# A gated cross-attention and quantised feed-forward block on one core: the variance and the joined statistics placed ahead of the last maximum, the roots kept in two buffers, the split alternated with longer operations, and the context halves turned at other places

## What is computed

```python
# attention: the mask and the shapes leave one key per query, so softmax is 1
x = x + tanh(g_xattn) * ((context @ Wv) @ Wout + bout)
# feed-forward, per token
h = layernorm(layernorm(x), ln1_g, ln1_b)
h = act_quant(h) @ weight_quant(w1).T + b1        # 256 -> 1024
h = gelu(h)
h = layernorm(h, ln2_g, ln2_b)
h = act_quant(h) @ weight_quant(w2).T + b2        # 1024 -> 256
x = x + tanh(g_ffn) * h
```

## Time and profile before

| what | value |
|---|---|
| median of 3 runs | 412.6 us (412.28 to 414.04) |
| the profiled execution | 411.33 us, span 409.5 us |
| busy: DVE, PE, ACT, POOL | 327.3 (80%), 309.5 (76%), 277.6 (68%), 221.4 (54%) us of the span |
| mean granted TensorE clock | 0.946 of full speed |

### The profile page before, as it was taken

The page is one execution under the profiler, slowest core; times in us unless marked ns, Lnnn a source line. Parts: engine busy times, 40 slices in busy tenths (PEclk is TensorE's granted clock), DMA queues, the critical chain, the costliest instruction groups (busy, mean ns, idle before and its releaser), DMA issues.

```text
span 409.5 us, 5758 instructions
## 1 busy us (share of the span) xinstructions
PE 309.5 (76%) x1658; PEld 186.5 (46%) x1658; DVE 327.3 (80%) x794; ACT 277.6 (68%) x446; POOL 221.4 (54%) x117
## 2 busy tenths in 40 slices
PE   2846777687969697979797969797979684938365
PEld 2744643343636363636363636363636341515043
DVE  0345461998999999999999999999999996968681
ACT  1202237598887878787888888787878776969421
POOL 4000416577566666666666666666666666664600
PEclk9988889998999999999999999999999996969688
DMA  7941223316365555556555555555552526353625
GB/s 225 378 149 47 81 91 108 89 51 115 117 116 169 113 170 112 171 104 182 108 175 107 178 105 179 103 179 104 128 101 81 101 79 88 93 96 86 153 53 154
DMA packets 98557, 51.59 MB, mean 126 GB/s; under 512 B 87407, under 2 KB 89640, under 8 KB 98526
## 3 DMA queue, kind: packets, MB, share of 16 engines
q1 hardware_dynamic: 96608, 51.00, 49.1%
q10 hardware_dynamic: 1918, 0.23, 0.4%
HBM read 21.78 MB, written 8.46 MB: 74 GB/s over the span
## 4 chain that ended last, share of the span: by engine, by line
DVE 41%; PE 30%; issue 12%; POOL 7%; DMA 5%; ACT 3%; DVEq 0%; POOLq 0%; ACTq 0%
DVE y L657 10%; PE bank_f L904 8%; POOL rstd L295 6%; PE slot_c L864 5%; DVE h L616 5%; DVE amax L624 5%; DVE res L707 5%; PE slot_a L890 4%; DVE amax L661 3%; DMA split_vectors<-vec_parts 3%; PE slot_b L890 3%; DVE x L573 2%; DVE parts L559 2%; PE slot_a L887 2%; PE bank_q L794 2%
## 5 line engine op out<-in xcount | busy, mean ns | idle before, releaser
L311 POOL TENSOR_TENSOR y<-u,g_bc 128x1024 f32<-128x1024 f32 x64 | 150.2, 2369 | 28.7 <-DVE parts L559 25.4
L295 POOL TENSOR_TENSOR rstd<-var,half_neg 128x8 f32<-128x8 f32 x18 | 30.3, 1683 | 129.5 <-DVE var L698 86.1
L657 DVE TENSOR_TENSOR y<-y,slot_c 128x1024 f32<-128x1024 f32 x64 | 77.6, 1212 | 5.0 <-PE slot_c L864 5.0
L661 DVE TENSOR_REDUCE amax<-y 128x1 f32<-128x1024 f32 x64 | 78.1, 1220 | 2.2
L441 ACT ACTIVATE junk<-u,usum 128x1024 bf16<-128x1024 f32 x64 | 73.7, 1151 | 1.2
L414 ACT ACTIVATE q<-y,s 128x1024 f16<-128x1024 f32 x64 | 69.8, 1139 | 5.2 <-DVE s L688 5.0
L843 PE MATMUL bank_q<-wvo,ctxT 128*128 128x256 f32 x256 | 69.1, 402 | 0.0
L904 PE MATMUL bank_f<-w2T,q2T 128*128 128x256 f16 x512 | 64.1, 281 | 0.0
L904 PEld LDWEIGHTS bank_f<-w2T,q2T 128*128 128x128 f16 x512 | 51.5, 101 | 14.3 <-issue 0.8
L405 ACT ACTIVATE q<-h,s 128x256 f16<-128x256 f32 x64 | 27.3, 496 | 41.2 <-DVE s L648 41.1
L864 PE MATMUL slot_c<-ln_rows,rows 128*128 128x512 bf16 x128 | 40.9, 402 | 16.9 <-DVE y L657 8.5
(11 more groups left out here) (104 smaller groups left out, 393.1 us busy)
## 6 DMA issues: line engine op xcount, KB each, us to landing
c_in<-in_ctx SPq DMA_DIRECT2D x16, 512.0 KB, 3.3
x_in<-in_x SPq DMA_DIRECT2D x16, 512.0 KB, 4.6
out<-res SPq DMA_DIRECT2D x32, 256.0 KB, 2.4
y<-in_L_ffn_w SPq DMA_DIRECT2D x2, 1024.0 KB, 12.1
u<-in_L_xattn_Wkv SPq DMA_DIRECT2D x1, 1024.0 KB, 7.0
u<-in_L_xattn_Wout SPq DMA_DIRECT2D x1, 1024.0 KB, 10.6
q2T<-q SPq DMA_TRANSPOSE x64, 3.3
g_bc<-in_L_ffn_ln_g SPq DMA_DIRECT2D x1, 512.0 KB, 12.4
```

The costliest lines, as they stand in the source:

```text
L295: nc.gpsimd.tensor_tensor(rstd[:, :, :], var[:, :, :], half_neg[:, :, :], ALU.pow) \
L311: nc.gpsimd.tensor_tensor(y[:, k % 2, t, :], u[:, t, :], g2_bc[:, :], ALU.mult).then_inc(gain2_done, 1)
L657: nc.vector.tensor_tensor(line, line, slot_c[:, :], ALU.add).then_inc(y_done, 1)
L661: nc.vector.tensor_reduce(amax2[:, t:t + 1], y[:, k % 2, t, :], AX.X, ALU.max, apply_absolute_value=True).then_inc(amax2_done, 1)
```

## The change

On DVE, `variance` works on block i at the end of body i, in place of block i-1 at the start of the next one. It and all of `join(i+2)` stand ahead of the maximum `first(i+1, 0)`, and the joins no longer lie among the steps of `first` and `second`. `rstd` has two buffers, `root(i+1)` is issued at the end of POOL's body i, and `deviations` is the first thing in a DVE body. The five splits alternate with residual, statistics and final operations. `final` is cut into single tiles, and those of block i-2 come after the fourth `row_max` in place of ahead of the fourth `row`. On PE the context half 0 is turned ahead of `hidden(0)`, half 1 after `shift_first`; `correction(3)` stands ahead of `second_product(i-2, 0)`. ACT copies half 0 ahead of `gelu(1)` and half 1 after `square(3)`.

```diff
-        rstd = sb("rstd", [P, 2, T])
+        rstd = sb("rstd", [P, 2, 2, T])
...
-                def root():
-
-                    wait(pool, var1_done, min(i + 2, S))
-                    wait(pool, var2_done, i)
-                    wait(pool, first_ready, min(i + 1, S))
-                    wait(pool, second_ready, i - 1)
+                def root(j):
+
+                    wait(pool, var1_done, min(j + 2, S))
+                    wait(pool, var2_done, j)
+                    wait(pool, first_ready, min(j, S))
+                    wait(pool, second_ready, j - 2)
...
                 if -1 <= i <= S:
-                    root()
                     wait(pool, split_steps, split_count(i))
...
+                if -1 <= i + 1 <= S:
+                    root(i + 1)
...
                 if live(i):
                     gelu(0)
                     square(0)
-                    gelu(1)
                 if live(i + 3) and i > -3:
                     take_context(i + 3, 0)
                 if live(i):
+                    gelu(1)
                     square(1)
                     gelu(2)
-                if live(i + 3) and i > -3:
-                    take_context(i + 3, 1)
-                if live(i):
                     square(2)
                     gelu(3)
                     square(3)
+                if live(i + 3) and i > -3:
+                    take_context(i + 3, 1)
...
                 def variance(k):
 
                     wait(dve, square_done, T * k + T)
-                    wait(dve, split_steps, split_count(k))
+                    wait(dve, std_done, i + 2)
+                    wait(dve, split_steps, split_count(i))
...
-                def final(k, pair):
-
-                    wait(dve, ffn_done, T * k + 2 * pair + 2)
-                    if pair == 0:
+                def final(k, t):
+
+                    if t % 2 == 0:
+                        wait(dve, ffn_done, T * k + t + 2)
+                    if t == 0:
                         wait(dve, stored[k % 2], 32 * (k // 2))
...
-                if live(i - 1):
-                    variance(i - 1)
+                splitting = -1 <= i <= S + 1
+                if -1 <= i <= S:
+                    deviations()
+                if splitting:
+                    split(0)
                 if live(i + 2):
                     residual(i + 2, 0)
+                if splitting:
+                    split(1)
+                if live(i + 2):
                     statistics(i + 2, 0)
...
-                if -1 <= i <= S:
-                    deviations()
-                if -1 <= i <= S + 1:
-                    for n in range(5):
-                        split(n)
+                if splitting:
+                    split(2)
+                if live(i + 2):
+                    statistics(i + 2, 1)
+                if splitting:
+                    split(3)
                 if live(i - 3):
-                    final(i - 3, 1)
+                    final(i - 3, 2)
+                if splitting:
+                    split(4)
+                if live(i - 3):
+                    final(i - 3, 3)
                 if live(i + 2):
                     residual(i + 2, 1)
-                    statistics(i + 2, 1)
+                    statistics(i + 2, 2)
+                    statistics(i + 2, 3)
...
-                if live(i - 2):
-                    final(i - 2, 0)
                 if live(i - 1):
                     row(i - 1, 3)
                     row_max(i - 1, 3)
+                if live(i - 2):
+                    final(i - 2, 0)
+                    final(i - 2, 1)
                 if live(i + 1):
                     shift_first(i + 1)
+                for n in range(4):
+                    if live(i + 2):
+                        join(i + 2, n)
+                if live(i):
+                    variance(i)
+                if live(i + 1):
                     first(i + 1, 0)
                 for n in range(4):
...
                     if live(i + 1):
                         first(i + 1, n + 1)
-                    if live(i + 2):
-                        join(i + 2, n)
...
+                if live(i + 3) and i > -3:
+                    turn_context(i + 3, 0)
                 if live(i):
                     hidden(0)
...
-                if live(i + 3) and i > -3:
-                    turn_context(i + 3, 0)
...
                 if live(i):
                     hidden(2)
+                if live(i - 1):
+                    correction(i - 1, 3)
                 if live(i - 2):
                     second_product(i - 2, 0)
-                if live(i + 3) and i > -3:
-                    turn_context(i + 3, 1)
-                if live(i - 1):
-                    correction(i - 1, 3)
                 if live(i):
                     hidden(3)
                 if live(i + 1):
                     shift_first(i + 1)
+                if live(i + 3) and i > -3:
+                    turn_context(i + 3, 1)
                 if live(i - 2):
                     second_product(i - 2, 1)
```

More of the change, by code:

```diff
@@ L288, in body @@
             def body(i):
-                def root():
-                    wait(pool, var1_done, min(i + 2, S))
-                    wait(pool, var2_done, i)
-                    wait(pool, first_ready, min(i + 1, S))
-                    wait(pool, second_ready, i - 1)
-                    nc.gpsimd.tensor_tensor(rstd[:, :, :], var[:, :, :], half_neg[:, :, :], ALU.pow) \
+                def root(j):
[3 more added lines that the diff above has]
+                    wait(pool, second_ready, j - 2)
+                    nc.gpsimd.tensor_tensor(rstd[:, j % 2, :, :], var[:, :, :], half_neg[:, :, :],
+                                            ALU.pow) \
                         .then_inc(rstd_done, 1)
@@ L541, in deviations @@
                     wait(dve, split_steps, split_count(i - 1))
-                    nc.vector.tensor_tensor(stat[:, 1:4:2, :], var[:, :, :], rstd[:, :, :], ALU.mult) \
+                    nc.vector.tensor_tensor(stat[:, 1:4:2, :], var[:, :, :], rstd[:, i % 2, :, :],
+                                            ALU.mult) \
                         .then_inc(std_done, 1)
@@ L577, in residual, with statistics @@
                         .then_inc(x1_done, 1)
[L579 to L585, removed]
+                def statistics(k, t):
+                    if t % 2 == 0:
+                        wait(dve, x1_done, 2 * k + t // 2 + 1)
+                        wait(dve, join_steps, 3 * k)
+                    op = nc.vector.bn_stats(bn[:, t, :], x1[:, k % SETS, t, :])
+                    if t == T - 1:
+                        op.then_inc(bn_done, 1)
                 def join(k, n):
                     if n == 0:
-                        wait(dve, bn_done, 2 * k + 2)
-                        wait(dve, split_steps, split_count(k - 2))
+                        wait(dve, bn_done, k + 1)
+                        wait(dve, std_done, i + 2)
+                        wait(dve, split_steps, split_count(i))
                         nc.vector.tensor_tensor(mean1[:, :], bn[:, :, 1], bn[:, :, 4], ALU.add)
@@ L627, in first @@
                         wait(dve, first_steps, 4 * k + 1)
-                        nc.vector.tensor_tensor(amax1_g[:, :], amax1[:, :], rstd[:, 0, :], ALU.mult) \
-                            .then_inc(first_steps, 1)
+                        nc.vector.tensor_tensor(amax1_g[:, :], amax1[:, :], rstd[:, i % 2, 0, :],
+                                                ALU.mult).then_inc(first_steps, 1)
                     elif n == 2:
@@ L648, in first @@
                         nc.vector.scalar_tensor_tensor(
-                            out=s1[:, :], in0=amax1_inv[:, :], scalar=QMAX * TINY, in1=rstd[:, 0, :],
-                            op0=ALU.mult, op1=ALU.mult).then_inc(first_ready, 1)
+                            out=s1[:, :], in0=amax1_inv[:, :], scalar=QMAX * TINY,
+                            in1=rstd[:, i % 2, 0, :], op0=ALU.mult, op1=ALU.mult).then_inc(first_ready, 1)
                 def row(k, t):
@@ L668, in second @@
                         wait(dve, amax2_done, T * k + those.stop)
-                        nc.vector.tensor_tensor(amax2_g[:, those], amax2[:, those], rstd[:, 1, those],
-                                                ALU.mult).then_inc(second_steps, 1)
+                        nc.vector.tensor_tensor(amax2_g[:, those], amax2[:, those],
+                                                rstd[:, i % 2, 1, those], ALU.mult).then_inc(second_steps, 1)
                     elif n == 1:
@@ L689, in second @@
                             out=s2[:, those], in0=amax2_inv[:, those], scalar=QMAX * TINY,
-                            in1=rstd[:, 1, those], op0=ALU.mult, op1=ALU.mult) \
+                            in1=rstd[:, i % 2, 1, those], op0=ALU.mult, op1=ALU.mult) \
                             .then_inc(second_ready, 1)
@@ L699, in variance @@
```

(11 more changed lines are left out.)

## The result

The changed kernel takes 414.13 us (median of 20 executions, 410.51 to 416.54) where the kernel before takes 412.37 (20, 410.18 to 414.11) on the same chip: 1.0043 times as long, 95% interval 1.0022 to 1.0064. So it is slower, by about 1.8 us (0.4%), and the forecast of 410.1 had the sign wrong, though 414.13 lies in the range. The profiled execution shows little of this. It took 411.29 us, one of the shortest of the 20, and its span of 409.5 us is that of before to the tenth.

A forecast was written before the change was run, and what follows sets the result against it. DVE was taken to bound the kernel, busy 19.32 of 20.56 us per steady body. Its terms gave 0.82, of which 0.58 kept; eleven bodies less 3.7 us at the ends made -2.7, forecast 410.1 us, range 407.0 to 414.5.

The forecast's parts named there:

- The steady body: Bodies 2 to 13: a body falls from 20.56 to 19.98 us, 0.58 less.
- Roots (0.36): DVE, steady body: with two root buffers L542 finds the root done, a gain of 0.36 us.
- finals (0.40): DVE, steady body: finals after the fourth maximum no longer wait for the second product, a gain of 0.40 us.
- the join alone: DVE, steady body: join without interleaving takes 0.90 us; join and variance alone together lose 0.51.
- residual(1) waits: DVE, steady body: residual(1) waits 0.4 us for the attention product, since residual(0) stands behind L542 and split(0).
- split alternated, 0.57: DVE, steady body: alternating splits with other operations hides latency between dependent steps, a gain of 0.57 us.
- Rival C: DVE: alternating hides nothing, 0.57 goes and a body gains only 0.2 us; 414.2 us; chance 0.08.
- Rival B: Steady body: last maximum waits for square(3) through the variance; body 20.57 us, 416 us, if ACT's chain keeps its length; chance 0.12.
- The ends: First and last bodies: losses of +1.9, +0.3, +0.8 and +0.7 us, 3.7 in all, against 11 body gains.
- The start, +1.9: Bodies 0 to 2: F(0) 3.0 us earlier, but the variance holds the maximum until square(3); F of body 3 1.9 later.
- The end, +1.8: From body 14 on: square(3) waits +0.3, row(0) of body 16 +0.8, last finals +0.7 us.
- 20.06, wanted at 20.29: Steady body: attention(i+3, 0), behind the moved context copy, ends at 20.06 us, in time for its use at 20.29.

The follow-up runs named there:

- e4_splits_together: Changed kernel with the five splits one behind the other again, after residual(0) and its statistics; 412.13 us, 0.9963 of the kernel before.
- t1_ends_splits_together: Changed kernel with bodies 0, 1 and the last from 14 on in the old order, and splits together in every body; 406.41 us, 0.9855 of before.
- e2_contexts_back: Changed kernel with the context halves turned and copied at their old places on PE and ACT; 429.33 us, 1.042 of the kernel before.
- e1_again: Changed kernel measured again without an edit; 414.13 us, 1.0038 of the kernel before.
- s1_start_as_before: Changed kernel with contexts, variance, joins and the steps behind the variance in the old order in bodies 0 and 1; 407.64 us, 0.9863 of before.

## Why the prediction was wrong

**The steady body: right in size, partly wrong in its reasons.** 19.98 us was forecast and is measured in every kernel with the changed middle. Roots (0.36) and finals (0.40) no longer wait, the join alone takes 0.91 (212.80 to 213.71) as read from the earlier trace rows, residual(1) waits 0.33 (forecast 0.4), and L702 starts with square(3) just done. But the term "split alternated, 0.57" bought nothing that was kept (`e4_splits_together`, `t1_ends_splits_together`): in both kernels row(0) starts 0.04 us after PE's correction behind ACT's take_rows ends (221.08 after, 221.14 in `e4_splits_together`), which the same section had placed at 4.81. The measured shares are 0.24 for the early variance with its root (less what the join by itself costs) and 0.28 for the finals and the second product; together with the contexts' 0.09 alone they make 0.61, near the 0.58. The contexts' share is 0.71 once the variance is early: they are what the early variance needs.

**Rival C.** The latency is real. In the steady body after, L561 to L575 is 0.12 us, L702 to L703 0.08, and the dependent L543 to L561 0.27. The prediction read the Trainium skill too narrowly here: VectorE: DVE Perf Modes, "The DRAIN you can't avoid", adds that an operation that is not held starts earlier, and the 0.12 and 0.08 agree with that. Where these rows differ from the Trainium skill is the semaphore, which by the same section costs nothing extra: a small operation that waits for the one before starts 0.27 us after it. The kernel gains nothing from either.

**Rival B** was held off only by the moved contexts. `e2_contexts_back` is this rival, and `e1_again` shows how near it is: 0.08 us lie between square(3) and L702.

**The failed step is "The ends".** It gave 3.7 us against the 11 gains of the middle (+1.9 at F of body 3, +0.3, +0.8, +0.7). By the medians it was about 8.1: 414.13 - 412.37 = +1.8, and 6.3 had been won in the middle. The profiles give the same: in the four with the changed start F(3) is at 118.1 in the mean, 4.5 us later than in the one of before (forecast 1.9), and in the two of the changed kernel F(14) to the end takes 3.6 longer (forecast 1.8). Both terms were too small:

- *The start, +1.9.* Two parts of it were seen: F(0) 3.0 earlier (in nine profiles with this order up to F(0), 53.46 to 57.15, mean 55.0, against 57.76 in the one of before: 2.8), and the variance holding the maximum in body 0 (1.86 us; the same wait forecast for body 1 isn't there). Given back from F(0) to F(3) were to be 4.9. It is 7.0 to 8.4 (62.85 and 64.26 less 55.85). The prediction placed attention(i+3, 0) behind the moved copy in a steady body, "20.06, wanted at 20.29", and didn't ask what that is in bodies 0 and 1, where PE has too little else: an idle PE (4.14 and 2.53 us), matmuls at the lower clock level, and a residual that waits. That cost is there twice. The maximum and the attention both wait for square(3), by two paths of about equal length, so that either half of the cure does nothing: from F(0) to F(3), 64.27 with the variance late, 62.84 with the contexts back, 62.85 and 64.26 with neither, and 59.12 with both.
- *The end, +1.8.* F(14) to the end of the span is 73.4 and 73.3 where before has 69.8: +3.6, of which 1.9 are there at row(0) of block 15 (forecast 1.1) and 1.7 come behind it (forecast 0.7). Variance(15) waits 2.13 us for square(3) and variance(14) 0.79. The 3.17 ahead of row(0) is no loss: before, 1.23 there came on top of 1.80 for the root. The finals of block 15 wait 2.62 and 4.44 for their products (before 3.87 and 2.31). The last of these products waits 0.72 us for a transpose, behind a split(4) that comes 0.5 us later than with the splits together, and runs at the lower level: 3.15 us for 16 matmuls, 1.91 at the higher one. Before, the product ahead of it was the slow one (3.31), so how much the level by itself costs at the end isn't shown.

**The median against the profile.** The prediction added the 1.3 us by which the median of before lies above its profiled execution. For the changed kernel it is 2.8, and `e1_again` was 1.8 on the other side. The two profiles of the changed kernel part ahead of bodies 0 and 1, between 30 and 40 us: the granted clock is 0.75 there in one and 0.51 in the other, and F(0) 3.4 us later. What the added waits of PE do to the scatter was not separated from that.

**What stays open.** From the profiles, the old end is worth some 4.6 us and the old start 4.3 (F(0) to F(3): mean 63.4 us in four profiles of the changed start, 59.1 in `s1_start_as_before`). By the ratios the end is worth 0.6%, 2.4 us, and the start 1.8%, 7.4 us, in both pairs of kernels. The sums, 8.9 and 9.8, are within what the intervals allow; the division is not, and why it differs was not settled, since one execution of each kernel leaves a trace.

## What to carry to other kernels

Cost a reordering of a software pipeline three times: in the steady body, in the bodies that fill it and in those that drain it, since a wait that row work covers in the middle stands bare there; here the order of 2 of 21 bodies costs 4 us by the profiles and 7 by the ratios, beside 6.3 gained in the steady ones. Give each stretch the order that suits it: with the old order in bodies 0, 1 and from 14 on the change is 2% faster than before, everywhere it is 0.4% slower. And undo suspected causes in pairs as well as singly, for two waits on one event hide each other.

## What was not expected of the hardware

The same program's executions differ together with PE's granted clock. The 20 executions of the changed kernel span 6.0 us, and the shortest two have clocks of 0.937 and 0.939, the longest two 0.923; the steady stretch, at 1.00, repeats to 0.01 us between profiles. After the same idle time of PE, 4.14 us, and the same matmuls in the 8 us before it, the first four matmuls of the attention took 1.91 us in one profile and 1.18 in another, with the lower level coming one group later there and staying longer.
